# Attention kernel on one core: each operand load of a head pair issued as two loads, one for each slot

## The chip, the cores and the metric

The kernel runs on one core of a Trainium2 chip. The metric is the device time of one execution in microseconds (us); lower is better. TensorE (PE), VectorE (DVE), ScalarE (ACT), GpSimd (POOL) and SyncE (SP) each run their own instruction stream and meet at semaphores. SP does no arithmetic here: it issues nearly all DMAs, in the order of its program.

## The reference

One transformer layer on x of shape 2 x 2048 x 256, with 16 heads of 16 dimensions. There are two causal attentions, whose outputs are mixed by a gate, then a layer norm, a gated feed-forward net and a second layer norm:

```python
q, k, v = qkv split of x @ qkv_w + qkv_b
std_logits = q . k * dh**-0.5                      # the "dot" logits, 16 numbers a head
write_lines = exterior(x_prev @ w1_write, x @ w2_write)   # 6 numbers a head, unit length
read_lines  = exterior(x @ w1_read, x @ w2_read)
geo_logits = read_lines . (write_lines @ J6) * inc_scale  # the "geo" logits
std_out = softmax(causal(std_logits)) @ v
geo_out = softmax(causal(geo_logits)) @ (x @ geo_w + geo_b)
gate = mean(sigmoid(x @ gate_w + gate_b))
x = layernorm(x + ((1 - gate) * std_out + gate * geo_out) @ out_w + out_b)
x = layernorm(x + (silu(x @ w_gate.T) * (x @ w_up.T)) @ w_down.T)      # weights are int / 127
```

## The kernel before

There are three stages, each a block that all engines enter and leave together.

**project** goes over 8 chunks of 512 tokens. PE multiplies x with the weights, DVE and ACT and POOL split every row of the queries, keys and lines into three bfloat16 parts, and SP stores the parts to HBM (`parts_geo`, `parts_dot`) and the values to `values`. A chunk has six row tiles, m = 0 to 5 (four of dot, two of geo). ACT may write the first part of row tile m of a chunk (line 666, `row_in`) only when the store of row tile m of the chunk before it has landed (`s_st[m]`, stored at line 504). After the four dot row tiles ACT takes the square root for the lengths of the lines (line 687, `nrm`), once a chunk; DVE needs it for the lines (line 801), and PE for turning these (line 629). So the times of line 687 are the beat of the stage.

SP's program in the last two chunks is written out: for each tt from 0 to 3 a store of values, a store of one row tile of the chunk before (tt = m), and then operand loads for item 0, so that these loads stand between the stores in SP's queue. In the first of the two rounds these are the 12 loads of dot, in the second the 12 loads of geo (two between each pair of stores, four of them after the two geo stores).

**attend** works on 16 items (a batch and a pair of heads). For every item PE needs operands in SBUF: `gq`, `gk` (geo) and `dq`, `dk` (dot), 128 partitions of 2048 bfloat16. `load_operands` brings them with 24 DMAs (index i: 12 of dot, then 12 of geo; a is the head of the pair, side is queries or keys, piece is which of three groups of slots). One of them fills 2 n partitions, with n = 16 rows (dot) or 6 rows (geo): two slots of n rows. For the queries and a piece other than the last, both slots get the same part. The three sets of operands are used in turn, and item it + 2 is loaded while item it runs; only item 1 is loaded whole at the start of the stage, ahead of everything else on SP.

The softmax needs the row maxima before the exponentials: PE computes maximum tiles for the next item (line 1091), DVE reduces them (lines 1250, 1253), and in two turns per item (EARLY, LATE; line 1125) they become rows, `mrow`, which SP puts into the query operands with four small DMAs per turn (line 911). PE waits for the early ones before it starts an item (`m_in[EARLY]`) and for the late ones before the last quarter of its steps. For item 0 the maxima are a prologue of their own. SP's program at the start of the stage is: 24 loads of item 1, the load of its values (line 969), the early `mrow` of item 0 as soon as DVE has written it, then the items.

**finish** does the output product, both norms and the feed-forward net; the change does not touch it.

Of the kernel before, what the change touches and what calls it, by code (L numbers as in the profile page):

```python
# [25 lines left out]
B, T, D, H = 2, 2048, 256, 16  # L26
# [20 lines left out]
GEO, DOT = 0, 1  # L47
# [14 lines left out]
DOT_MINOR = 2 * DH  # L62
DOT_ROWS = (DOT_MAIN, DOT_MINOR + 2)
LOADS = 12
VW = 32
NSET = 3

# [143 lines left out]
def build(nc, xt, x, w_qk, b_qk, w_v, w_line, b_v, b_gate, inc, out_w, out_b, wg, wu, wd, out):  # L211
    ctx = ExitStack()
    with ctx:
        parts = (nc.dram_tensor("parts_geo", (2, B, NPART, H * NCOMP, T), BF16).ap(),
                 nc.dram_tensor("parts_dot", (2, B, NPART, H * DH, T), BF16).ap())
        values = nc.dram_tensor("values", (ITEMS, P, NKB, NBLK * VW), F32).ap()
        raw = nc.dram_tensor("raw", (B, 2, H * VW, T), F32).ap()
        gates = nc.dram_tensor("gates", (2, B * T), F32).ap()
# [47 lines left out]
def operand_set(sb, sem, i):  # L266

    return {"geo": [sb(f"g{x}{i}", [P, T], BF16) for x in "qk"],
            "dot": [sb(f"d{x}{i}", [P, 2, T], BF16) for x in "qk"],
            "v": sb(f"va{i}", [P, NKB, NBLK * VW]),  # L270
            "geo_in": sem(f"geo_in{i}"), "dot_in": sem(f"dot_in{i}"), "v_in": sem(f"v_in{i}")}


def load_operands(q, parts, it, to, which=range(2 * LOADS)):

    b, g = it // PAIRS_OF_HEADS, it % PAIRS_OF_HEADS
    for i in which:
        kind, a, side, piece = DOT - i // LOADS, (i // 6) % 2, (i // 3) % 2, i % 3
        n = (NCOMP, DH)[kind]
        dst = to[("geo", "dot")[kind]][side]  # L280
        minor = piece == 2
        row = HALF * a + (4 * n * minor if kind == GEO else 0)
        first = g * (2 * n) + a * n
        slot = FIRST_SLOT[side][minor]
        if side == 0 and not minor:
            src = parts[kind][0, b, slot + piece, bass.ds(first, n), :].unsqueeze(0).to_broadcast([2, n, T])
        else:
            src = parts[kind][side, b, slot:slot + 2, bass.ds(first, n), :]
        row += 0 if minor else 2 * n * piece
        rows = dst[row:row + 2 * n, :] if kind == GEO else dst[row:row + 2 * n, int(minor), :]  # L290
        q.dma_start(rows, src).then_inc(to[("geo_in", "dot_in")[kind]], 16)


def load_den(q, raw, gates, b, late):

    q.dma_start(late["den"][:, :], raw[b].rearrange("k (h v) t -> (k h) v t", v=VW)[:, DH, :]
                .rearrange("r (s t) -> r s t", t=CH)).then_inc(late["den_in"], 16)
# [20 lines left out]
def load_att(q, raw, rden, c, par, late):  # L318

    b, cols = c // CPB, bass.ds((c % CPB) * CH, CH)  # L320
    for kind in range(2):
        for k in range(NK):
            rows = raw[b, kind, k * 8 * VW:(k + 1) * 8 * VW, cols].rearrange("(h v d) t -> v h d t", v=2, d=DH)
            q.dma_start(late["att"][par][:, kind, k, :], rows[0]).then_inc(late["att_in"][par], 16)
# [79 lines left out]
def project(nc, xt, w_qk, b_qk, w_v, w_line, b_v, b_gate, inc, parts, values, sets, fixed,  # L404
# [9 lines left out]
    with ExitStack() as ctx:  # L414
        def sb(name, shape, dt=F32):
            return ctx.enter_context(nc.sbuf_tensor(name, shape, dt))
# [15 lines left out]
        xc = [sb(f"xc{i}", [P, NK, CH + 1]) for i in range(2)]  # L432
        vn = [sb(f"vn{i}", [P, 2 * H, VW]) for i in range(TT)]
        gs = sb("gs", [P, 2, TT * 2, H * 4])
# [44 lines left out]
        def _(q):  # L479
# [57 lines left out]
            for tt in range(TT):  # L537
                store_v(NC - 2, tt)
                store_row(NC - 3, tt)
                load_operands(q, parts, 0, sets[0], range(2 * tt, 2 * tt + 2))  # L540
            for m in range(4, NR):
                store_row(NC - 3, m)
                load_operands(q, parts, 0, sets[0], range(2 * m, 2 * m + 2))
            for tt in range(TT):
                store_v(NC - 1, tt)
                store_row(NC - 2, tt)
                load_operands(q, parts, 0, sets[0], range(12 + 2 * tt, 14 + 2 * tt))
# [280 lines left out]
def attend(nc, parts, values, raw, gates, ident, mask_qk, gate_z, wide, out_w, out_b, wg, wu, wd, weights,  # L828
           sets, fixed, rden, x, late):
    with ExitStack() as ctx:  # L830
# [9 lines left out]
        sets = sets + [operand_set(sb, sem, 2)]  # L840
# [196 lines left out]
        def _(pe):  # L1037
# [26 lines left out]
            def bank_free(it, i):  # L1064

                j, earlier = RING.owner(i)
                if isinstance(it, int) and it < 0 and (earlier or j < RING.head):
                    return
                at = it - 1 if earlier else it
                part = RING.part[j]  # L1070
                if part is None:
                    pe.wait_ge(mx_free, RING.freed(at, j))
                else:
                    pe.wait_ge(mrow_ready[part], item_of(at, part) + 1)

            def max_tiles_of(it, to, h):

                _, which, use = to
                q_set, k_set = sets[which]["dot"]
                if h == LEAD:  # L1080

                    pe.wait_ge(sets[which]["dot_in"], (use + 1) * LOADS * 16)
                at, last = 0, [None, None]
                for u in MAX_IN[h]:
                    qb, k0, w, _ = MAXT[u]
                    for a in range(2):
                        i = RING.place[h, a]
                        if not at:
                            bank_free(it, i)
                        rows = slice(HALF * a, HALF * a + DOT_MAIN)  # L1090
                        last[a] = pe.matmul(mx[:, RING.bank[i], at:at + w], q_set[rows, 0, qb * P:(qb + 1) * P],  # L1091
                                            k_set[rows, 0, k0:k0 + w], start=True, stop=True)
                        if u == MAX_IN[h][-1]:
                            last[a].then_inc(mx_ready, 1)
                    at += w

            def wide_pair(to, part, n, u):
                nit, which, use = to
                q_set, k_set = sets[which]["geo"]
                if n == 0:  # L1100
                    pe.wait_ge(sets[which]["geo_in"], (use + 1) * LOADS * 16)
                else:

                    pe.wait_ge(wx_free[part], nit * len(PART_TILES[part]) + n)
                qb, k0, w, _ = MAXT[u]
                for a in range(2):
                    rows = slice(HALF * a, HALF * a + GEO_ROWS)
                    last = pe.matmul(mx[:, a, 0:w], q_set[rows, qb * P:(qb + 1) * P], k_set[rows, k0:k0 + w],
                                     start=True, stop=True)
                last.then_inc(wx_ready[part], 1)  # L1110
# [44 lines left out]
            def step(at, before, nxt, s, head):  # L1155

                it, which, use = at
                groups = len(STEPS[s][1])

                def earlier(h):  # L1160
                    if h >= BEHIND:
                        times_v(*at, *PVS[h - BEHIND], head)
                    elif before is not None:
                        times_v(*before, *PVS[h - BEHIND], head)

                for j in range(groups):
                    h = PV_AT[s, j]
                    to = at if h < LEAD else nxt
                    scores(it, which, s, j, GEO, head)
                    if to and MAX_IN[h]:  # L1170
                        max_tiles_of(it, to, h)
                    scores(it, which, s, j, DOT, head)
                    if not nxt and (s, j) in PRODUCT_AT:
                        tt = PRODUCT_AT.index((s, j))

                        pe.wait_ge(late["mix_ready"], 1)
                        if tt >= MX_RING:
                            pe.wait_ge(late["sums_ready"], tt - MX_RING + 1)
                        first_product(pe, tt, mx[:, tt % MX_RING, 0:D], late["mix"][0], weights["out"], late)
                    earlier(h)  # L1180
                    if to and h in TURN:
                        turn(it, to, TURN.index(h))

            def item(at, before, nxt, head):

                it, which, use = at
                pe.wait_ge(sets[which]["geo_in"], (use + 1) * LOADS * 16)
                pe.wait_ge(m_in[EARLY], (it + 1) * 64)
                for s in range(NSTEP):
                    if s == FIRST_OF[PARTS[LATE][0]]:  # L1190
                        pe.wait_ge(m_in[LATE], (it + 1) * 64)
                    step(at, before, nxt, s, head)
# [16 lines left out]
            pe.wait_ge(fixed, 2 * FIXES)  # L1209
            prologue()  # L1210
            item(static(0), None, static(1), True)

            pe.wait_ge(fixed, NSET * FIXES)
            for it in range(1, ITEMS):
                item(static(it), static(it - 1), static(it + 1) if it < LAST_ITEM else None, False)
# [498 lines left out]
```

## Time and profile before

| | |
|---|---|
| time, median of 3 runs | 1713.91 us (1712.94 to 1715.13) |
| the profiled execution's own time | 1713.8 us |
| its span, first to last instruction | 1712.1 us |
| project | 0 to about 210 us |
| attend | about 210 to 1399 us |
| finish | about 1399 us to the end |
| mean granted TensorE clock | 0.967 |

The profile is of one execution. Line numbers are those of the kernel before. For SP the trace shows the time that each DMA-issuing instruction held SP's queue; a DMA's data moves later. A share of DMA is the mean over the core's 16 DMA engines.

### The profile page before, as it was taken

What the parts mean: (1) busy time and instruction counts of PE and PEld (TensorE: products, weight loads), DVE (VectorE), ACT (ScalarE), POOL (GpSimd) and SP (SyncE); (2) the same over time, 40 slices, a digit from 0 to 9 for tenths busy, and PEclk for the clock granted to TensorE, in tenths of its full rate; (3) what the DMA queues carried; (4) which work ended last, traced back from release to release, by engine and by line L of the source; (5) the groups of instructions that cost most, each with busy time, mean ns of one, the idle gap of its engine ahead of it and who ended that gap; (6) DMA issues with size and microseconds to landing.
All of it is one profiled execution on the core that took longest, in us unless ns stands there. A gap on an engine that the chain in (4) does not pass through costs nothing. (4 is left out here: it accounts for less than half of the span.)

```text
span 1712.1 us, 31671 instructions
## 1 busy us (share of the span) xinstructions
PE 1597.8 (93%) x11809; PEld 560.2 (33%) x11809; DVE 1073.9 (63%) x2580; ACT 1196.7 (70%) x1409; POOL 334.2 (20%) x479
## 2 busy tenths in 40 slices
PE   8997269999999999999999999999999989999997
PEld 4554112222222222222222222222222235555564
DVE  4885386766677676776777667677676335544433
ACT  2442208999999999999998999999999951211211
POOL 4442311212121121211211112111121323211000
PEclk9998658999999999999999999999999999999999
DMA  5884521321212212122121221212213023222000
GB/s 172 249 252 154 184 73 42 89 90 50 89 51 69 73 50 72 50 69 73 49 83 52 69 73 50 73 49 69 74 54 114 22 82 132 74 74 86 12 13 25
DMA packets 95579, 140.31 MB, mean 82 GB/s; under 512 B 6352, under 2 KB 64528, under 8 KB 93360
## 3 DMA queue, kind: packets, MB, share of 16 engines
q1 hardware_dynamic: 94208, 135.08, 23.9%
q0 software_dynamic: 624, 2.75, 0.6%
q8 instruction: 97, 1.59, 0.4%
q14 instruction: 74, 0.61, 0.1%
q10 hardware_dynamic: 576, 0.28, 0.1%
HBM read 81.96 MB, written 55.61 MB: 80 GB/s over the span
## 5 line engine op out<-in xcount | busy, mean ns | idle before, releaser
L1234 ACT ACTIVATE prob<-ex 128x1024 f32<-128x1024 f32 (+1 forms) x1152 | 1055.4, 976 | 127.6 <-PE ex L1053 110.6
L1253 DVE TENSOR_REDUCE mp<-mx 128x1 f32<-128x512 f32 x768 | 493.1, 685 | 201.9 <-PE mx L1091 201.8
L1148 PE MATMUL pv<-prob,va 128*32 128x512 f32 (+3 forms) x5120 | 588.4, 541 | 1.7 <-POOL prob L1021 0.4
L1021 POOL TENSOR_SCALAR_AFFINE_SELECT prob<-prob 128x256 f32<-128x256 f32 (+1 forms) x384 | 185.4, 483 | 966.5 <-ACT prob L1234 961.5
L1059 PE MATMUL ex<-dq,dk 34*128 34x512 bf16 (+7 forms) x2560 | 335.8, 348 | 7.9 <-ACT prob L1234 2.2
L1250 DVE CUSTOM_DVE_ANT_0 dull<-mx,mask_qk 128x128 f32<-128x128 f32 (+3 forms) x512 | 223.2, 488 | 98.4 <-PE mx L1091 98.2
L1091 PE MATMUL mx<-dk,dq 64*128 64x512 bf16 (+3 forms) x1280 | 227.6, 357 | 17.9 <-issue 10.4
L1053 PE MATMUL ex<-gq,gk 38*128 38x512 bf16 (+3 forms) x1280 | 218.9, 355 | 10.0 <-DMA dq<-mrow 8.7
L1053 PEld LDWEIGHTS ex<-gq,gk 38*128 38x128 bf16 x1280 | 56.5, 93 | 417.7 <-ACT prob L1234 363.4
L1148 PEld LDWEIGHTS pv<-prob,va 128*32 128x32 f32 x5120 | 108.5, 108 | 232.8 <-issue 186.6
L1577 ACT ACTIVATE sg<-pg 128x512 f32<-128x512 f32 x48 | 28.7, 597 | 219.4 <-PE pg L1517 219.1
L1059 PEld LDWEIGHTS ex<-dq,dk 64*128 64x128 bf16 (+1 forms) x2560 | 93.6, 94 | 165.4 <-ACT prob L1234 132.8
L1517 PE MATMUL pg<-y_t,wg_f 128*128 128x512 f32 x192 | 90.5, 594 | 1.1 <-ACT y_t L1560 1.1
L1533 PE MATMUL po<-wd_f,ht 128*128 128x256 f32 x384 | 85.0, 381 | 5.9 <-DVE ht L1645 5.9
L577 POOL TENSOR_TENSOR sp<-d,sp 128x512 bf16<-128x512 f32 (+1 forms) x48 | 66.7, 1400 | 120.9 <-ACT sp L672 120.3
L1517 PE MATMUL pg<-y_t,wu_f 128*128 128x512 f32 x192 | 90.2, 592 | 0.0
L596 PE MATMUL pn<-wv,xc 128*128 128x512 f32 x128 | 63.9, 624 | 20.1 <-ACT gz L683 12.0
L1645 DVE SCALAR_TENSOR_TENSOR ht<-pg,sg 128x512 f32<-128x512 f32 x48 | 33.0, 690 | 78.7 <-ACT sg L1577 78.7
L1091 PEld LDWEIGHTS mx<-dk,dq 64*128 64x128 bf16 x1280 | 64.8, 96 | 53.4 <-issue 17.2
L1533 PEld LDWEIGHTS po<-wd_f,ht 128*128 128x128 f32 x384 | 72.3, 190 | 17.9 <-issue 5.1
L1320 DVE COPY on<-pv 128x512 f32<-128x512 f32 x64 | 44.2, 691 | 39.9 <-PE pv L1148 37.8
L666 ACT ACTIVATE sp<-pr,bqs 128x512 bf16<-128x512 f32 x32 | 21.9, 683 | 57.7 <-DMA parts_dot<-sp 46.7
(108 smaller groups left out, 906.7 us busy)
## 6 DMA issues: line engine op xcount, KB each, us to landing
values<-vn SPq DMA_DIRECT2D x32, 512.0 KB, 5.2
va<-values SPq DMA_DIRECT2D x16, 1024.0 KB, 18.6
raw<-on SPq DMA_DIRECT2D x64, 256.0 KB
parts_dot<-sp SPq DMA_DIRECT2D x32, 384.0 KB, 5.4
dq<-parts_dot SPq DMA_DIRECT2D x96, 128.0 KB
dk<-parts_dot SPq DMA_DIRECT2D x96, 128.0 KB
parts_geo<-sp SPq DMA_DIRECT2D x16, 288.0 KB, 5.4
gq<-parts_geo SPq DMA_DIRECT2D x96, 48.0 KB
```

The lines of the kernel that those rows point to most:

```text
L577: g.tensor_tensor(out=sp3[m][0:n, SLOTS[m][2], :], in0=d32[m][0:n, :], in1=sp3[m][0:n, SLOTS[m][1], :], op=ALU.subtract).then_inc(p3_done, 1)
L596: last = pe.matmul(bank[:, 0, :], xc[par][:, k, tok], wv[:, k, :], start=k == 0, stop=k == NK - 1)
L1021: g.affine_select(out=cut, in_=cut, compare_op=ALU.is_ge, fill=0.0, base=0, pattern=[[0, nb], [1, P]], channel_multiplier=-1).then_inc(mas ...
L1053: last = pe.matmul(ex[:, n % 2, a * CH + at:a * CH + at + w], k_set[rows, keys], q_set[rows, queries], start=True, stop=True)
L1059: last = pe.matmul(ex[:, n % 2, a * CH + at:a * CH + at + w], k_set[rows, part, keys], q_set[rows, part, queries], start=part == 0, stop=p ...
L1091: last[a] = pe.matmul(mx[:, RING.bank[i], at:at + w], q_set[rows, 0, qb * P:(qb + 1) * P], k_set[rows, 0, k0:k0 + w], start=True, stop=True)
L1148: last = pe.matmul(pv[blk * VW:(blk + 1) * VW, CH - w:CH], sets[which]["v"][:, kb, blk * VW:(blk + 1) * VW], prob[UNIT_AT[s, j, kind] % NP ...
L1234: act.activation(prob[n % NPROB][:, :].rearrange("p (b c) -> p b c", b=2)[:, :, 0:w], ex[:, n % 2, :].rearrange("p (b c) -> p b c", b=2)[: ...
L1250: return v.tensor_tensor_reduce(out=scrap, in0=source, in1=mask_qk[:, CH - w:CH], scale=1.0, scalar=3 * MASKED, op0=ALU.add, op1=ALU.max, ...
L1253: return v.tensor_reduce(out=to, in_=source, axis=AX.X, op=ALU.max)
L1517: last = pe.matmul(pg[m % 2][:, i, :], w[:, k, m * P:(m + 1) * P], y_t[:, k, :], start=k == 0, stop=k == NK - 1)
L1533: last = pe.matmul(po[tt % 2][:, 0:D], ht[:, m, tt * P:(tt + 1) * P], wdf[:, m, :], start=m == 0, stop=m == NM - 1)
```

## The change

Every DMA of `load_operands` becomes two, one for each of its two slots. Each has n rows of 2048 elements as its source and n partitions as its destination, and the row count is its outermost count; before, the source's outermost count was the 2 of the slots (a stored dimension or a broadcast). An item takes 48 loads: 24 of 64 KB (dot, 16 rows) and 24 of 24 KB (geo, 6 rows), in place of 12 of 128 KB and 12 of 48 KB. The bytes, their places in SBUF and the order of the pieces stay. The waits on the loads count twice as many increments. The loads stand in the same places of SP's program.

```diff
+LOADED = 2 * LOADS * 16
...
-        if side == 0 and not minor:
-            src = parts[kind][0, b, slot + piece, bass.ds(first, n), :].unsqueeze(0).to_broadcast([2, n, T])
-        else:
-            src = parts[kind][side, b, slot:slot + 2, bass.ds(first, n), :]
         row += 0 if minor else 2 * n * piece
-        rows = dst[row:row + 2 * n, :] if kind == GEO else dst[row:row + 2 * n, int(minor), :]
-        q.dma_start(rows, src).then_inc(to[("geo_in", "dot_in")[kind]], 16)
+        for j in range(2):
+
+            from_slot = slot + piece if side == 0 and not minor else slot + j
+            rows = slice(row + j * n, row + (j + 1) * n)
+            to_rows = dst[rows, :] if kind == GEO else dst[rows, int(minor), :]
+            q.dma_start(to_rows, parts[kind][side, b, from_slot, bass.ds(first, n), :])\
+             .then_inc(to[("geo_in", "dot_in")[kind]], 16)
...
-                    pe.wait_ge(sets[which]["dot_in"], (use + 1) * LOADS * 16)
+                    pe.wait_ge(sets[which]["dot_in"], (use + 1) * LOADED)
...
-                    pe.wait_ge(sets[which]["geo_in"], (use + 1) * LOADS * 16)
+                    pe.wait_ge(sets[which]["geo_in"], (use + 1) * LOADED)
...
-                pe.wait_ge(sets[which]["geo_in"], (use + 1) * LOADS * 16)
+                pe.wait_ge(sets[which]["geo_in"], (use + 1) * LOADED)
```

## Rows read from the trace of the kernel before

**Rows 1.** The page: busy time of PE, share of the span.
```profile
PE 1597.8 (93%) x11809; PEld 560.2 (33%) x11809; DVE 1073.9 (63%) x2580; ACT 1196.7 (70%) x1409; POOL 334.2 (20%) x479
```

**Rows 2.** PE's waits, 285 to 1390 us: total, times, longest.
```profile
PE mx L1091 <- DVE mp L1253: 2.0, 1, 2.0
```

**Rows 3.** ACT's timeline, line 687: start, duration, instruction, wait before it.
```profile
108.94 0.31 ACT L687 ACTIVATE nrm<-ss 128x128 f32<-128x128 f32 x1 [0.56 <-DVE ss L797]
128.22 0.31 ACT L687 ACTIVATE nrm<-ss 128x128 f32<-128x128 f32 x1 [0.85 <-DVE ss L797]
161.80 0.30 ACT L687 ACTIVATE nrm<-ss 128x128 f32<-128x128 f32 x1
194.04 0.30 ACT L687 ACTIVATE nrm<-ss 128x128 f32<-128x128 f32 x1
```

**Rows 4.** SP's timeline, stores of dot row tiles in project.
```profile
120.67 1.40 SPq L504 DMA_DIRECT2D parts_dot<-sp  x1
...
133.90 0.37 SPq L504 DMA_DIRECT2D parts_dot<-sp  x1
...
151.08 4.32 SPq L504 DMA_DIRECT2D parts_dot<-sp  x1
...
167.26 2.97 SPq L504 DMA_DIRECT2D parts_dot<-sp  x1
...
185.58 1.58 SPq L504 DMA_DIRECT2D parts_dot<-sp  x1
```

**Rows 5.** ACT's timeline, the first parts that waited for stores.
```profile
161.21 0.69 ACT L666 ACTIVATE sp<-pr,bqs 128x512 bf16<-128x512 f32 x1 [6.83 <-DMA parts_dot<-sp]
...
193.46 0.69 ACT L666 ACTIVATE sp<-pr,bqs 128x512 bf16<-128x512 f32 x1 [3.71 <-DMA parts_dot<-sp]
```

**Rows 6.** DMA view, 60 to 130 us: KB each, median us to landing.
```profile
parts_dot<-sp SPq DMA_DIRECT2D x14, 384.0 KB, 5.2
```

**Rows 7.** DMA view, 130 to 210 us, the same columns.
```profile
parts_dot<-sp SPq DMA_DIRECT2D x12, 384.0 KB, 8.0
```

**Rows 8.** Windows: length, busy us of each engine, clock, DMA share, GB/s.
```profile
100.00:137.00 37.00, 37.00 (x137) 21.85 (x136) 32.27 (x50) 16.77 (x38) 16.67 (x12) 1.00 0.80 241
...
211.00:241.00 30.00, 22.63 (x51) 4.25 (x51) 27.78 (x83) 1.15 (x2) 7.39 (x5) 0.50 0.13 51
...
245.00:259.00 14.00, 4.86 (x10) 0.71 (x7) 6.11 (x13) 0.00 (x0) 0.00 (x0) 0.50 0.22 73
259.00:275.00 16.00, 15.42 (x110) 3.95 (x110) 9.30 (x15) 12.10 (x14) 2.89 (x6) 0.69 0.13 51
```

**Rows 9.** SP's timeline at the start of attend.
```profile
210.24 1.96 SPq L291 DMA_DIRECT2D dq<-parts_dot  x3
...
240.94 1.02 SPq L969 DMA_DIRECT2D va<-values  x1
...
247.67 2.02 SPq L911 DMA_DIRECT2D dq<-mrow  x1
```

**Rows 10.** The timeline of all engines there: the rows of maxima.
```profile
239.19 0.29 DVE L1312 CAST mrow<-mx 96x128 bf16<-96x128 f32 x1 [0.57 <-PE mx L1125]
```

**Rows 11.** PE's timeline: end of the prologue, item 0, a later item.
```profile
246.18 4.21 PE L1091 MATMUL mx<-dk,dq 64*128 64x512 bf16 x7 [0.52 <-DVE mp L1250]
259.07 0.61 PE L1053 MATMUL ex<-gq,gk 38*128 38x512 bf16 x2 [8.68 <-DMA dq<-mrow]
...
280.78 0.33 PE L1125 MATMUL mx<-ident,negm 128*128 128x128 f32 x1
...
351.08 0.33 PE L1125 MATMUL mx<-ident,negm 128*128 128x128 f32 x1
```

**Rows 12.** Issues by source line: min/median/max ns on SP, first and last start.
```profile
L291 SPq DMA_DIRECT2D dq<-parts_dot x96: 597/640/3367, 134.3 to 1211.6; - x96
L291 SPq DMA_DIRECT2D dk<-parts_dot x96: 597/1234/3945, 141.2 to 1216.1; - x96
```

**Rows 13.** The same for line 504, the stores.
```profile
L504 SPq DMA_DIRECT2D parts_dot<-sp x32: 372/1176/4322, 36.8 to 202.8; - x32
```

## The prediction, made before the changed kernel was run

> **What bounds the kernel now.** I read the page first: PE is busy 93% of the span [rows 1], so a transfer can only matter where PE stands still. The list of PE's waits over the attention stage from 285 to 1390 us has four entries; the largest is one wait of 2.0 us, for DVE [rows 2], and none is for a DMA. There the loads are hidden, two items ahead, and an item takes 351.08 - 280.78 = 70.3 us [rows 11]. That leaves the ends of the stages.
>
> In project the beat is the square root on ACT. It comes 19.28 us after the one before (128.22 - 108.94), as long as SP only stores; the two rounds in which SP also issues the loads of item 0 take 33.58 us (161.80 - 128.22) and 32.24 us (194.04 - 161.80) [rows 3]. ACT's timeline says why: it waits for stores of row tiles, 6.83 us before 161.21 and 3.71 before 193.46, and the square root follows directly [rows 5]. SP's timeline says what these stores do: the last dot store of the first round begins at 151.08 and holds SP for 4.32 us, where an unhindered one takes 0.37 [rows 4], and from issue to landing a store takes 8.0 us in this stretch, 5.2 before it [rows 6, 7]. The two rounds lose (33.58 - 19.28) + (32.24 - 19.28) = 14.3 + 13.0 = 27.3 us.
>
> At the start of attend SP issues the 24 loads of item 1 from 210.24 to 240.94, 30.7 us or 1.28 each, and the early rows of maxima only behind them, until 249.69 [rows 9], though DVE had them at 239.48 [rows 10]. PE ends its prologue at 246.18 + 4.21 = 250.39 and stands until 259.07; the last 8.68 us of PE's idle time end with the landing of `mrow` [rows 11].
>
> **One cause for both.** From 211 to 241 us, when nothing but operand loads moves, the DMA share is 0.13 at 51 GB/s [rows 8]. 2/16 is 0.125: the old load, with its outermost count of 2, keeps two of the 16 DMA engines busy, at some 26 GB/s each. Item 1's loads are 12 x 128 + 12 x 48 KB = 2.16 MB, 42 us at that rate; stores that use all 16 engines must stand behind the loads on two of them, and so must `mrow`. In the rounds without loads DMA moves 241 GB/s at a share of 0.80 [rows 8], about 300 at a full share.
> The Trainium skill has this as a rule (DMA: Bandwidth & Descriptors, the section Why a DMA increments its semaphore by 16 and not by 1): the largest number up to 16 that divides the outermost counts of both sides gives the number of engines. The trace agrees for 2. By the rule the new dot loads would run on 16 engines and the geo loads on 6.
>
> **The change part by part.**
> 1. *Issues.* 24 more per item. What a load on more engines holds SP for, no row shows. The nearest from below is a store at 0.37 us, spread over 128 partitions [rows 13]; from the other side the old load at its least, 0.60 [rows 12]. I take 0.60 for all 48, which also covers some queueing; the far bound is 1.23, the median of the `dk` loads, which were held up by full queues [rows 12]. In the middle of attend the issues then take 48 x 0.60 = 29 us of SP's 70.3 per item; cost nothing, because PE waits for no transfer there. If SP needed over 70 us, each item would be longer.
> 2. *First round with loads.* Row tile 0 can be stored at 133.90 as now, since POOL gives it [rows 4]. Until the store of row tile 3 SP has 12 loads (7.2 us) and 5 more stores, for which I take 0.9 us each, between 0.37 and the 1.40 of a busy stretch [rows 4]: 133.90 + 0.4 + 7.2 + 4.5 = 146.0. Landing 5.2 later [rows 6] is 151.2, and 0.7 for the first part gives a square root at 151.9 in place of 161.80: gain 9.9. Bounds: no better than the beat, 14.3; worse if the landing stays at 8.0 [rows 7], 7.
> 3. *Second round.* Row tile 0 can be stored 167.26 - 161.80 = 5.46 us after the square root [rows 3, 4]. Then 0.4 + 7.2 + 5 x 0.65 (SP's queue is less full, the geo loads are small) puts row tile 3's store at 16.3, its landing at 21.5 and the next square root at 22.2 after the last, in place of 32.24: gain 10.0. Bounds: 13.0, the beat, and 6 (landing 8.0, more per store).
> 4. *End of project.* The load of item 0's values, 1 MB, today lies before the last six stores; moved nearer to them it takes 3.4 us at 300 GB/s, a part of which can delay them: -1 (0 to -2).
> 5. *Start of attend.* Everything here is 20 us earlier. SP begins at 190.3; 48 x 0.60 = 28.8 gives 219.1, the values 0.4 to 1.0 more, about 220. The rows of maxima are there at 239.48 - 19.9 = 219.6, so SP comes just in time. Four issues at 0.6 and a landing of up to 5.2 end at 227.8, before PE ends its prologue at 250.39 - 19.9 = 230.5. What PE then waits for is nothing but its own order: gain 8.5 of the 8.68. At 0.8 us a load SP would be 9.6 us later and the gain about 2; that is the lower bound.
> 6. *The clock.* The granted clock is at the lower level (0.50) from before the prologue until some 20 us after the first item begins [rows 8]. PE idles shorter but still idles between the stages. In 259 to 275 the mean is 0.69 over 15.42 busy us [rows 8]; if that stretch ran at full clock it would save up to 0.31 x 15.42 = 4.8 us, if the low stretch lasted as much longer it would cost about the same. I take 0.
> 7. *What PE and the others compute,* the bytes, and finish do not change: 0.
>
> Sum: 9.9 + 10.0 - 1 + 8.5 = 27.4 us. The profiled execution took 1713.8 us, 1.7 more than its span, and is within 0.1 of the median 1713.91; 1713.9 - 27.4 = 1686.5.
>
> **Rivals.**
> *A. The other side: SP becomes the bound.* Let c be the time that one load holds SP. Steps 2 and 3 lose 12 (c - 0.6) each. In step 5 the first item can begin at 48 c + 6.5 us (values, `mrow`, landing) after the stage does. With (19.9 - 24 (c - 0.6)) from project, the net is 259.07 - 210.24 - 6.5 + 19.9 + 14.4 - 72 c = 76.6 - 72 c, so it decides at c = 1.06. With c = 1.23 it gives 12 us slower, about 1726, and SP would be issuing for 59 of 70.3 us of every item. For it: the median of `dk` is 1.23. Against it: those were held up by two full queues, and the minimum of 0.60 stands where the queues were empty [rows 12].
> The Trainium skill speaks for this side (DMA: Bandwidth & Descriptors, the sections Anatomy of one DMA and Rules for kernel authors): small transfers should be coalesced, below 64 KB they are mostly overhead, with about 2.0 us fixed for each. If these followed one another, 48 would fill 96 us of a 70.3 us item. Against that, the old loads already follow each other every 0.60 us at best [rows 12], so the fixed part overlaps.
> *B. The loads do not spread* (the engine count is set by something else than the outermost count). Then two engines still carry 2.16 MB in 42 us at the start of attend, and only issues are added: within 0.2%, about 1714. Against: 0.13 fits a count of 2 too well.
> *C. Half of it.* The stores in the tail of project still queue: a round with the dot loads must move some 241 GB/s x 19.28 us + 1.6 MB = 6.2 MB, 21 us at 300 GB/s, and if its landings come at the end of that, or if SP reaches `mrow` late, the gain is 8 to 17: about 1701.
> *D. All of it:* both rounds at the beat (27.3), the start (8.5) and some of the clock: 36 to 40, about 1676.
>
> **How the numbers follow.** My forecast (1678 to 1695) 0.62, D 0.12, C 0.15, B 0.04, A 0.07. I predict 1686.5. The range for 8 in 10 goes to D's near side and takes most of C: 1674 to 1700. What can be told from no change is about 0.2%, 3.4 us; faster by more 0.89, within 0.04, slower 0.07.
>
> **What would show it.** In the changed kernel's profile the square roots of line 687's kind should be about 24 and 22 us apart in the last two rounds, in place of 33.6 and 32.2; the dot stores in SP's timeline should hold SP under 1.5 us each; in the first 20 us of attend the DMA share should exceed 0.13 in bursts, with loads following each other at 0.4 to 0.6 us; PE's wait ahead of the first item should be under 1 us and no longer end with `mrow`; the item period should stay 70.3 us. I am wrong if a single load holds SP for over 1 us with empty queues (A), if the DMA share stays at 0.13 (B), or if PE shows waits for DMAs in the middle of attend.

## The result, and the profile after

The changed kernel takes 1682.88 us (median of 4 runs, 1682.28 to 1683.22), against 1714.52 us for the kernel before on the same chip (4 runs, 1712.94 to 1715.73). The ratio is 0.9817, with a 95% interval of 0.9802 to 0.9832: 31.6 us faster. The forecast was 1686.5 us. The profiled execution has a span of 1681.1 us, against 1712.1 before. Lines below the changed function are numbered two higher than before.

ACT's timeline in project, the square roots, against [rows 3] (start, duration, instruction, wait before it):

```profile
128.64 0.31 ACT L689 ACTIVATE nrm<-ss 128x128 f32<-128x128 f32 x1 [0.81 <-DVE ss L799]
151.22 0.30 ACT L689 ACTIVATE nrm<-ss 128x128 f32<-128x128 f32 x1
172.93 0.30 ACT L689 ACTIVATE nrm<-ss 128x128 f32<-128x128 f32 x1
```

The two rounds with loads now take 151.22 - 128.64 = 22.58 us and 172.93 - 151.22 = 21.71 us, in place of 33.58 and 32.24. They are still longer than the 19.28 of a round without loads.

Windows of these two rounds (length, busy us of PE, PEld, DVE, ACT, POOL, clock, DMA share, GB/s); the kernel before has a share of 0.48 and 0.52 in its two:

```profile
128.64:151.22 22.58, 22.32 (x85) 13.21 (x84) 16.88 (x26) 9.04 (x21) 8.57 (x6) 1.00 0.80 232
151.22:172.93 21.71, 14.08 (x48) 7.49 (x48) 15.69 (x24) 8.92 (x22) 8.56 (x6) 0.95 0.81 243
```

SP's timeline, the dot stores of these rounds (with the 12 loads ahead of row tile 3's store in the first), the start of attend and the rows of maxima, against [rows 4, 9]:

```profile
134.32 0.37 SPq L506 DMA_DIRECT2D parts_dot<-sp  x1
134.74 2.04 SPq L292 DMA_DIRECT2D dq<-parts_dot  x4
...
137.99 2.37 SPq L292 DMA_DIRECT2D dq<-parts_dot  x2
140.40 0.89 SPq L292 DMA_DIRECT2D dk<-parts_dot  x2
...
142.48 3.26 SPq L292 DMA_DIRECT2D dk<-parts_dot  x4
...
146.37 0.51 SPq L506 DMA_DIRECT2D parts_dot<-sp  x1
...
156.70 0.40 SPq L506 DMA_DIRECT2D parts_dot<-sp  x1
...
167.97 0.51 SPq L506 DMA_DIRECT2D parts_dot<-sp  x1
...
189.62 2.65 SPq L292 DMA_DIRECT2D dq<-parts_dot  x6
...
208.86 0.36 SPq L971 DMA_DIRECT2D va<-values  x1
218.95 0.84 SPq L913 DMA_DIRECT2D gq<-mrow  x1
```

The last dot store of the first round starts at 146.37 in place of 151.08, and holds SP for 0.51 us in place of 4.32. From issue to landing a store of a dot row tile takes 4.3 us here (DMA view, 130 to 210 us), in place of the 8.0 of [rows 7]:

```profile
parts_dot<-sp SPq DMA_DIRECT2D x12, 384.0 KB, 4.3
```

At the start of attend SP issues twice as many loads in 19.2 us (189.62 to 208.86), where the 24 old ones took 30.7. Then it issues nothing for 9.7 us, until DVE has written the rows of maxima.

The same by source line (min/median/max ns that one issue held SP), against [rows 12]:

```profile
L292 SPq DMA_DIRECT2D dq<-parts_dot x192: 318/420/1772, 134.7 to 1175.8; - x192
...
L292 SPq DMA_DIRECT2D gq<-parts_geo x192: 262/295/1215, 157.1 to 1214.3; - x192
```

Windows at the start of attend (length, busy us of PE, PEld, DVE, ACT, POOL, clock, DMA share, GB/s), the first while dot loads are issued, the second while geo loads are; against [rows 8]:

```profile
190.00:200.00 10.00, 7.28 (x21) 1.50 (x21) 8.20 (x31) 1.53 (x2) 7.69 (x7) 0.50 0.51 135
200.00:209.00 9.00, 8.99 (x16) 1.51 (x15) 9.00 (x18) 0.00 (x0) 0.00 (x0) 0.50 0.32 88
```

PE's timeline around the first item, against [rows 11]:

```profile
225.55 4.21 PE L1093 MATMUL mx<-dk,dq 64*128 64x512 bf16 x7 [0.52 <-DVE mp L1252]
229.25 0.94 PE L1055 MATMUL ex<-gq,gk 38*128 38x512 bf16 x2
...
251.28 0.33 PE L1127 MATMUL mx<-ident,negm 128*128 128x128 f32 x1
```

The share of DMA is no longer held at 0.13, and the first item follows the prologue with no wait in brackets, where it used to follow 8.68 us of waiting for `mrow`. Put together: the rounds give 11.0 + 10.5 us. From the last square root to the start of attend takes 189.62 - 172.93 = 16.69 us (before 210.24 - 194.04 = 16.20), which costs 0.5. From there to the first item takes 229.25 - 189.62 = 39.63 (before 48.83), which gives 9.2. That is 30.2 us. The square root at which this sum begins came 0.4 later here, and from the first item to the end it is 1681.1 - 229.25 = 1451.9 in place of 1453.0, 1.2 less. Together these make the 31.0 us by which the spans differ.

### The profile page after: what moved, and what is told of

Read it like the earlier page. It is cut to its first block and busy times, and to the rows that moved or that the text cites. A ratio compares the mean times of both kernels' runs of the same rounds, so it can differ in the third digit from the quotient of the medians.

```text
span 1681.1 us, 32055 instructions
## 1 busy us (share of the span) xinstructions
PE 1593.9 (95%) x11809; PEld 558.9 (33%) x11809; DVE 1071.4 (64%) x2580; ACT 1196.1 (71%) x1409; POOL 334.4 (20%) x479
## 5 line engine op out<-in xcount | busy, mean ns | idle before, releaser
L1093 PE MATMUL mx<-dk,dq 64*128 64x512 bf16 (+3 forms) x1280 | 227.9, 356 | 18.6 <-issue 10.9
L1616 DVE SCALAR_TENSOR_TENSOR sums<-po,y 128x256 f32<-128x256 f32 x32 | 13.6, 425 | 69.2 <-PE po L1535 69.2
```

## The experiments

Two theories were to be told apart. **S**: a load with an outermost count of 2 keeps only two engines' worth of DMA busy (a share of 0.13), and what is issued behind it waits; the gain is the spreading. **H**: the gain comes from halving the loads, so that SP gives shorter pieces and gets back to its stores sooner. Intervals are 95% intervals of the ratio to the kernel before, run on the same chip.

**The outermost count alone, 2.** All is as in the changed kernel, but the source is two blocks of rows that lie apart. `COUNT` is 2 for both kinds here; in the next run it is 6 for geo and 8 for dot.

```diff
-            q.dma_start(to_rows, parts[kind][side, b, from_slot, bass.ds(first, n), :])\
+            c = COUNT[kind]
+            heads = parts[kind][side, b, from_slot].rearrange("(k r) t -> k r t", r=n)
+            head = min(first // n, H - c)
+            q.dma_start(to_rows, heads[head:head + c, 0:n // c, :])\
```

> The changed kernel with its 48 loads, but each load's source is written as 2 blocks of n/2 rows that lie apart, so that its outermost count is 2 again. Packets, bytes and destination stay; the blocks come from the rows of other heads, so the output is not the layer's. Theory S (the gain comes from spreading a load over more DMA engines): the gain is gone. The loads at the start of attend move at about 51 GB/s and a share of 0.13 again, the first item starts after the rows of maxima land, and the time is 1714 to 1722 us. Theory H (the gain comes from halving the loads, with shorter pieces between the stores): the time stays within 3 us of 1683.

Measured: 1717.07 us, ratio 1.0013 (1.0003 to 1.0023). The gain is gone. The window while item 1 is loaded, and SP's and PE's timelines there:

```profile
212.00:240.00 28.00, 21.42 (x44) 3.90 (x43) 27.14 (x77) 0.00 (x0) 4.82 (x3) 0.50 0.13 53
```

```profile
246.13 2.33 SPq L917 DMA_DIRECT2D dq<-mrow  x1
```

```profile
257.65 0.61 PE L1059 MATMUL ex<-gq,gk 38*128 38x512 bf16 x2 [8.99 <-DMA dq<-mrow]
```

The share is 0.13 and the rate 53 GB/s as before, with 48 loads of half the size. SP has issued the last row of maxima at 248.46, and still PE starts only at 257.65: these 9 us are the landing of the rows behind the loads, not SP's issues. The rounds are back at 32.7 and 32.3 us.

**The outermost count alone, 8 and 6.**

> As count2, with 8 blocks of 2 rows for dot and 6 blocks of 1 row for geo; again other heads' rows are read. Theory S: nearly all of the gain stays, since 8 engines move 64 KB in about 0.3 us, less than an issue takes: 1683 to 1688 us, with the loads limited by their issue. If an issue costs more because the source has one dimension more, it holds SP for about 0.6 us as the old loads did, and for 0.42 if only the size or the number of engines counts. Theory H: 1683 as well.

Measured: 1688.57 us, ratio 0.9850 (0.9832 to 0.9867), 0.6 us above the expected range. Most of the gain is back with nothing altered but the counts. H is refuted by this pair. Part of what is missing against the changed kernel is the issue: with the added dimension one dot load holds SP for 0.657 us (median), while the geo loads, which have kept their two dimensions, take 0.295 as in the changed kernel:

```profile
L296 SPq DMA_DIRECT2D dq<-parts_dot x192: 657/657/1296, 133.7 to 1181.7; - x192
...
L296 SPq DMA_DIRECT2D gq<-parts_geo x192: 272/295/1267, 159.4 to 1219.0; - x192
```

The rounds are 24.9 and 24.1 us here, 2.3 longer each; for the first, 12 loads x (0.657 - 0.420) = 2.8 answers to it. In the second, SP comes to the first store 6.4 us after the square root in place of 5.5, and the 12 geo loads ahead of row tile 3's store hold SP for 9.0 us in place of 7.8, though their median is the same; what lengthened these is not settled.

**Halves by columns, count still 2.**

```diff
-        q.dma_start(rows, src).then_inc(to[("geo_in", "dot_in")[kind]], 16)
+        for j in range(2):
+            cols = slice(j * (T // 2), (j + 1) * (T // 2))
+            q.dma_start(rows[:, cols], src[:, :, cols]).then_inc(to[("geo_in", "dot_in")[kind]], 16)
```

> The kernel before with each of its loads cut into two by columns: 48 loads of half the size, but the outermost count stays 2 and the rows of a packet are 2 KB in place of 4 KB. Theory S: no gain; the two engines have as much to do or a little more, and 24 more issues come on top: 1714 to 1725 us. Theory H: about 1683.

Measured: 1724.32 us, ratio 1.0045 (1.0028 to 1.0062), slower than the kernel before. In the profile, 3.3 us of the loss lie before the first item (262.36 in place of 259.07, with a wait for `mrow` of 10.44 us) and 8.5 after it. Among PE's waits from 285 to 1340 us is an entry of which the kernel before has 0.9 us:

```profile
PE ex L1056 <- issue: 6.4, 6, 2.2
```

These stand at the starts of items, where PE waits for operands and rows of maxima. The profile names no releaser ("issue"), so that the loads cause them is likely, but not shown.

**One place at a time.** The new form only for item 0 (the tail of project), only for item 1 (the start of attend), only for items 2 to 15 (the middle), the old form elsewhere.

> The new form for the loads of item 0 alone (the two rounds of project), the old form for all others. Theory S by place: the two rounds gain 21 us, the rows of maxima wait behind item 1's loads as before: 1692 to 1695 us.

> The new form for item 1 alone (the start of attend), the old form for all others. By place: 9 to 9.5 us gained, 1704 to 1706 us, if the two places are independent of each other.

> The new form for items 2 to 15 alone. By place: these loads are hidden before and after, so no difference: 1713 to 1715.5 us. If freed queues help the middle of attend, some us faster.

Measured: 1695.42 us, ratio 0.9892 (0.9877 to 0.9907); 1705.71 us, 0.9952 (0.9938 to 0.9965); 1714.68 us, 1.0004 (0.9995 to 1.0013). Against the 1714.04 us of the kernel before beside them these are 18.6, 8.3 and -0.6 us. The first is 0.4 us above its expected range, the other two are inside. Both places are shown, and the middle gives nothing by itself. The run with item 0 alone keeps the wait at the start of attend, the run with item 1 alone has none (PE's timelines):

```profile
240.10 0.61 PE L1073 MATMUL ex<-gq,gk 38*128 38x512 bf16 x2 [9.26 <-DMA dq<-mrow]
```

```profile
249.78 0.93 PE L1073 MATMUL ex<-gq,gk 38*128 38x512 bf16 x2
```

The three sum to 26.3 us, 5 less than the whole change. The profiles show the shortfall on both sides of the first item's start. After it, the time to the end is 1694.4 - 240.10 = 1454.3 us with item 0 alone, 1454.9 with item 1 alone and 1452.9 with the middle alone, against 1453.0 before and 1451.9 in the changed kernel. Ahead of it, PE's wait for `mrow` is longer than the 8.68 us of before where item 1 keeps the old form: 9.26 us with item 0 alone, and with the middle alone:

```profile
260.90 0.61 PE L1073 MATMUL ex<-gq,gk 38*128 38x512 bf16 x2 [11.03 <-DMA dq<-mrow]
```

What makes these differences is not settled.

**96 loads.** Each load of the changed kernel cut once more, by columns, and still spread.

> The changed kernel with each load cut once more, by columns: 96 loads an item, still spread over 16 and 6 engines. It doubles the issues. If an issue takes what it takes now (0.42 us for dot, 0.30 for geo), an item's loads hold SP for 35 us of 70, the middle of attend stays as it is, the two rounds of project lose up to 12 x 0.4 = 5 us together, and the 17 us of SP time of item 1's loads become 35, which ends later than the rows of maxima (about 10 us after the loads end now) by some 7 us: the first item starts 0 to 8 us later. Time 1684 to 1697 us. The rival A of the prediction (issues decide) needs over 1714.

Measured: 1707.39 us, ratio 0.9955 (0.9939 to 0.9972), 24 us slower than the changed kernel: my range was wrong. The median issue takes what it took (0.420 and 0.295 us), but I had counted the effect on the rounds too low. ACT's timeline gives rounds of 27.8 and 31.2 us:

```profile
128.62 0.31 ACT L691 ACTIVATE nrm<-ss 128x128 f32<-128x128 f32 x1 [0.83 <-DVE ss L801]
156.39 0.30 ACT L691 ACTIVATE nrm<-ss 128x128 f32<-128x128 f32 x1
187.59 0.30 ACT L691 ACTIVATE nrm<-ss 128x128 f32<-128x128 f32 x1
```

The first is 5.2 us longer than in the changed kernel, to which 12 loads x 0.42 = 5.0 answer. SP's timeline shows the reason for the second:

```profile
162.55 3.73 SPq L294 DMA_DIRECT2D dk<-parts_dot  x8
...
166.92 0.51 SPq L508 DMA_DIRECT2D parts_dot<-sp  x1
```

Row tile 0 of the second round could be stored 5.5 us after the square root, at 161.9, but SP is still issuing loads of the first round and comes to it at 166.92. The 12 further loads between the stores add their issues on top. At the start of attend 96 loads hold SP from 206.98 to 247.1 us, past the rows of maxima, and PE waits for `mrow`, with a DMA share of 0.28 from 210 to 230 us. The last row of maxima and PE's first matmul of the item:

```profile
249.84 0.61 SPq L915 DMA_DIRECT2D dq<-mrow  x1
```

```profile
253.47 0.61 PE L1057 MATMUL ex<-gq,gk 38*128 38x512 bf16 x2 [6.35 <-DMA dq<-mrow]
```

Here PE starts 3.0 us after SP has issued the last row, where the run with count 2 took 9.2. This is the mechanism of the prediction's rival A, reached with the issues in place of the price of one.

**The order.** First all loads of item 0 behind the ten stores of their round:

> The changed kernel with the loads of item 0 issued behind the ten stores of their round in place of between them. The stores of row tiles 1 to 3 no longer wait for SP to issue loads: if that and not DMA bandwidth makes the two rounds 22.6 and 21.7 us long in place of 19.3, they become 19.3 to 20.5, and the time 1678 to 1681 us. If the bandwidth decides, it stays within 1 us of 1683; the loads then meet the next round's stores.

Measured: 1685.70 us, ratio 0.9837 (0.9824 to 0.9851): no gain, where 1678 to 1681 was expected. ACT's timeline:

```profile
127.53 0.31 ACT L683 ACTIVATE nrm<-ss 128x128 f32<-128x128 f32 x1 [0.81 <-DVE ss L793]
146.81 0.31 ACT L683 ACTIVATE nrm<-ss 128x128 f32<-128x128 f32 x1 [0.77 <-DVE ss L793]
171.19 0.30 ACT L683 ACTIVATE nrm<-ss 128x128 f32<-128x128 f32 x1
```

The first round is at the beat, 19.28 us, as the expectation had it. The second takes 24.38: SP issues the first round's loads until 156.25, and comes to row tile 0 at 156.92, 4.6 us after it could be stored. And the end of project takes 190.99 - 171.19 = 19.8 us in place of 16.7, since loads and values now stand before its stores. Three runs followed beside a repetition of the changed kernel. In the first, item 0's geo loads and values are issued in attend; in the second its dot loads are also divided, half behind the stores of each round. The second's edit (lines taken out of project not shown):

```diff
+            for c in (NC - 2, NC - 1):
+                for tt in range(TT):
+                    store_v(c, tt)
+                    store_row(c - 1, tt)
+                for m in range(4, NR):
+                    store_row(c - 1, m)
+                first = 6 * (c - (NC - 2))
+                load_operands(q, parts, 0, sets[0], range(first, first + 6))
...
-            load_operands(q, parts, 1, sets[1])
+            load_operands(q, parts, 1, sets[1], range(0, 12))
+            load_operands(q, parts, 0, sets[0], range(12, 24))
+            q.dma_start(sets[0]["v"][:, :, :], values[0]).then_inc(sets[0]["v_in"], 16)
+            load_operands(q, parts, 1, sets[1], range(12, 24))
```

> The changed kernel once more, unaltered, beside the three that follow on the same chip: 1682 to 1684 us.

> The changed kernel with item 0's geo loads and its values taken out of project and issued at the start of attend, between item 1's dot and geo loads, where SP now stands idle for 10 us before the rows of maxima. The second round then has no loads in it and should take 19.3 to 20 us in place of 21.7, the end of project up to 1 us less; the 24 geo loads take SP 7 us of its 10 idle ones, so the first item still starts in time: 1679 to 1681.5 us. If SP's idle time isn't enough, the first item waits for the rows of maxima and the gain is eaten.

> As geo_late, and the dot loads of item 0 divided: half of them behind the ten stores of the first of the two rounds, half behind those of the second. From the run with all loads behind the stores, its first round was at the beat (19.28) and its second lost 5 us because SP still issued loads when the next stores were due; 12 loads take 5 to 7 us, which end before. Both rounds 19.3 to 20, so attend starts 4 to 6 us earlier than in the changed kernel: 1676 to 1679.5 us. If DMA bandwidth decides, about 1680 or more.

> The order of the run before with the old loads, 24 for an item on two engines. If the place between the stores were the cause in project and not the two engines, the rounds would be near 19.3 here too. By theory S the first round is at 19.3 to 21, the second longer, as stores queue behind the 12 MB-eighths on two engines (0.77 MB, 15 us), and at the start of attend 2.7 MB on two engines take 53 us, so that the first item starts some 10 us later than in the kernel before relative to the start of the stage: 1705 to 1722 us in all.

Measured:

| | us | ratio to the kernel before |
|---|---|---|
| changed kernel again | 1683.15 | 0.9812 (0.9798 to 0.9825) |
| geo loads in attend | 1678.30 | 0.9794 (0.9781 to 0.9808) |
| and dot loads divided, behind the stores | 1676.53 | 0.9772 (0.9759 to 0.9786) |
| the same order with the old loads | 1717.96 | 1.0022 (1.0013 to 1.0032) |

With only the geo loads moved, 0.7 us better than expected, the first round stays at 22.4 us and the second falls to 19.4. The third row is the fastest kernel of the study, 6.6 us faster than the changed one. In its ACT timeline both rounds are at the beat:

```profile
128.36 0.31 ACT L682 ACTIVATE nrm<-ss 128x128 f32<-128x128 f32 x1 [0.77 <-DVE ss L792]
147.63 0.31 ACT L682 ACTIVATE nrm<-ss 128x128 f32<-128x128 f32 x1 [0.75 <-DVE ss L792]
166.81 0.31 ACT L682 ACTIVATE nrm<-ss 128x128 f32<-128x128 f32 x1 [0.28 <-DVE ss L792]
```

They take 19.27 and 19.18 us, and its windows show that more was moved per microsecond than in the changed kernel's rounds (232 and 243 GB/s):

```profile
128.36:147.63 19.27, 19.27 (x73) 11.44 (x73) 16.26 (x26) 9.15 (x21) 8.57 (x6) 1.00 0.81 248
147.63:166.81 19.18, 16.59 (x62) 9.37 (x60) 16.21 (x25) 9.15 (x21) 8.57 (x6) 1.00 0.87 259
```

SP is done with everything in front of the rows of maxima 0.6 us before they are there, so its idle time is used up (SP's timeline):

```profile
209.40 0.60 SPq L967 DMA_DIRECT2D va<-values  x1
210.57 0.84 SPq L906 DMA_DIRECT2D gq<-mrow  x1
```

With the old loads the same order loses at once what it wins: the first round is 19.3 us, but the second 27.9, and PE waits at the start of attend:

```profile
263.20 0.61 PE L1049 MATMUL ex<-gq,gk 38*128 38x512 bf16 x2 [23.62 <-DMA dq<-mrow]
```

With the old loads the order only moves the queue.

## Why the prediction was right

*Steps 2 and 3, the two rounds.* Forecast 9.9 and 10.0, measured 11.0 and 10.5. The path held: row tile 3's store waits for SP's queue, its landing for ACT. The size came out in part by luck. The store was to start at 146.0 and started at 146.37, but of the 12.05 us from row tile 0's store to it, the 12 loads took 8.6 in place of 7.2 (0.71 each), the five stores 2.2 in place of 4.5, and 0.9 lie between issues, which I had not counted. In the second round the loads took 7.8 in place of 7.2 (0.65 each), the stores 2.25 in place of 3.25. The stores also landed in 4.3 us in place of the 5.2 that I took from the undisturbed rounds. For what remains above the beat I held bandwidth possible (rival C). The fastest kernel has both rounds at the beat at 248 and 259 GB/s, more than the changed kernel moves in its longer ones. So it is SP's order and issue time; why an issue is longer among the stores than the 0.42 and 0.295 us of attend is not settled, and the traffic of the stores may have a part in that.

*Step 5, the start of attend.* Forecast 8.5, measured 9.2. Right in the mechanism, but for another reason in the detail: SP was to come just in time for the rows of maxima, and it came 10 us early. The start of attend that I took, 190.3, left out the 1 us of step 4; it came at 189.62.

*Step 1, the price of an issue,* is the term that was mis-sized. I took 0.60 us, the old load's least, as a cautious value; a new dot load took 0.42 and a new geo load 0.295. The 48 issues at the start of attend took 19 us in place of 28.8. That did not carry into the sum, because PE's own prologue ends later than either. In the rounds 0.60 was too low, as said above.

*Step 4* was forecast at -1, measured -0.5. *Step 6, the clock,* at 0: from the first item to its late turn it takes 251.28 - 229.25 = 22.0 us in place of 280.78 - 259.07 = 21.7, no gain. *Step 7 and the middle of attend* at 0: the run with items 2 to 15 alone gives -0.6 us, within its interval of no change.

*Rivals.* B, that the loads don't spread, is excluded by the share and by the pair of runs on the count. D needs both rounds at the beat, which only the run with divided loads reached. A did not occur with 48 loads, and the run with 96 shows that it is real: its two places (stores behind issues, rows of maxima behind issues) both came back. The fixed time for each transfer, of which A's paragraph speaks, did not add up: at the start of attend 48 loads were issued in 19.2 us, 0.40 each. The 3.6 us between forecast (1686.5) and result (1682.9) are 2.8 from steps 2 to 5 (30.2 against 27.4) and 1.2 from the time after the first item, less the 0.4 by which the first square root came later. Step 7 had put the 1.2 at nothing.

## What to carry to other kernels

Look at the share of DMA in a stretch where a single kind of transfer moves: here a constant 0.13, close to 2/16, went with an outermost count of 2 at two sizes of load, and stores and small transfers issued behind such loads were held up. Such a load was free in the steady state and still cost at the ends of stages, where stores or small transfers are queued behind it; price it there. Once the loads were spread, the issuing engine's time was the next limit: put loads where that queue is idle, and cut them no finer than the spreading needs.

## What the runs showed of the hardware

The time that an issue held SP went with the form of the pattern and not with the bytes. Loads whose two sides are both rows of 2048 or 1024 elements took 0.420 us at the median with 16 rows (64 or 32 KB) and 0.295 with 6 rows (24 or 12 KB). Rows and engines change together between these two, so the runs do not tell which of them makes the difference. Where the source of a load had one dimension more than its destination, the least was 0.597 for 2 x 16 rows in the old kernel and for 2 x 8 rows in the run with count 2, 0.594 for 2 x 3 rows, and 0.657 for 8 x 2 rows. So at count 2 the number of rows made no difference, and for the same 16 rows a count of 8 took 0.06 more than a count of 2: a small part that grows with the engines is not excluded. A third dimension alone is not what costs. The stores of dot row tiles have three dimensions on both sides and held SP for 0.37 us at the least, while the rows of maxima, with two in the source and three in SBUF, took 0.607:

```profile
L506 SPq DMA_DIRECT2D parts_dot<-sp x32: 372/506/1395, 37.2 to 181.7; - x32
...
L913 SPq DMA_DIRECT2D dq<-mrow x64: 607/612/639, 219.8 to 1311.2; - x64
```

So writing a load with its rows outermost paid twice here: the transfer was spread, and two issues of the new form (0.84 us for dot, 0.59 for geo) cost SP little more, or no more, than one of the old form with an empty queue. In the rounds of project, among the stores, the same issues were longer (0.71 and 0.65 us each on average).
